# The row maxima of the first pair of sequences are spread from 16 rows instead of 128

## The reference, cut to what matters

```python
def _mlstm_parallel(q, k, v, i_pre, f_pre):
    log_fg = jax.nn.log_sigmoid(f_pre)
    lf_cs = jnp.cumsum(log_fg, axis=-1)
    lf = jnp.concatenate([jnp.zeros_like(lf_cs[..., :1]), lf_cs], axis=-1)
    log_d = lf[..., 1:, None] - lf[..., None, 1:] + i_pre[..., None, :]
    log_d = jnp.where(mask, log_d, -jnp.inf)
    m = jnp.max(log_d, axis=-1, keepdims=True)
    d_mat = jnp.exp(log_d - m)
    scores = jnp.einsum('bhtd,bhsd->bhts', q, k) * (1.0 / np.sqrt(DH))
    s_mat = scores * d_mat
    ...
x = x + _L0_xattn_ref(_layernorm(x), ctx_1024, ctx_1024, ifgate_w, ifgate_b, outnorm_w)
x = x + _L0_ffn_ref(_layernorm(x), w1_w, w1_s, w2_w, w2_s, h1_w, h1_s, h2_w, h2_s, w3_w, w3_s)
```

## Time and profile before

| | us |
|---|---|
| median of 3 runs | 836.69 |
| lowest and highest of the 3 | 834.64, 836.72 |
| the profiled execution | 834.64 |
| its span in the trace | 832.7 |
| PE busy | 807.9 (97% of the span) |
| DVE busy | 558.6 (67%) |
| ACT busy | 376.0 (45%) |
| POOL busy | 47.7 (6%) |

### The profile page before, as it was taken

The page is one execution under the profiler, slowest core; times in us unless marked ns, Lnnn a source line. Parts: engine busy times, 40 slices in busy tenths (PEclk is TensorE's granted clock), DMA queues, the critical chain, the costliest instruction groups (busy, mean ns, idle before and its releaser), DMA issues.

```text
span 832.7 us, 11915 instructions
## 1 busy us (share of the span) xinstructions
PE 807.9 (97%) x4666; PEld 687.8 (83%) x4666; DVE 558.6 (67%) x1336; ACT 376.0 (45%) x546; POOL 47.7 (6%) x53
## 2 busy tenths in 40 slices
PE   8886999999999999999999999999999999999996
PEld 6685888888888788888888888888888888888886
DVE  6865866659594785758685695858767582965543
ACT  3303544647235554546345562455545472335331
POOL 3100002000010002000020001100020000000000
PEclk9967999999999999999999999999999999999998
DMA  9922000220012100040012200031001300350540
GB/s 341 358 91 89 1 26 27 92 112 26 5 48 120 59 26 27 26 178 1 26 51 102 76 26 28 26 138 42 26 27 50 129 1 1 127 177 1 171 133 27
DMA packets 14027, 63.24 MB, mean 76 GB/s; under 512 B 1952, under 2 KB 2320, under 8 KB 11152
## 3 DMA queue, kind: packets, MB, share of 16 engines
q1 hardware_dynamic: 12672, 50.91, 17.5%
q0 software_dynamic: 1296, 11.53, 3.5%
HBM read 53.94 MB, written 8.50 MB: 75 GB/s over the span
## 4 chain that ended last, share of the span: by engine, by line
PE 79%; DVE 12%; issue 1%; ACT 1%
PE ps_f L1212 22%; PE ps_f L1213 22%; DVE decay L778 7%; PE ps_f L1188 7%; PE ps_f L1189 7%; PE ps_a L1151 6%; PE ps_f L1245 4%; PE ps_f L1246 4%; DVE decay L794 2%; PE ps_a L1131 2%; PE ps_a L1039 2%; PE ps_a L1140 1%; PE ps_a L1161 1%; PE ps_a L1102 1%; PE ps_a L1095 1%
## 5 line engine op out<-in xcount | busy, mean ns | idle before, releaser
L1212 PE MATMUL ps_f<-h_hi,wgt 128*128 128x512 f32 x1024 | 404.1, 395 | 0.0
L1213 PE MATMUL ps_f<-h_lo,wgt 128*128 128x512 f32 x1024 | 399.1, 390 | 0.0
L1212 PEld LDWEIGHTS ps_f<-h_hi,wgt 128*128 128x128 f32 x1024 | 192.4, 188 | 40.2 <-issue 0.3
L1213 PEld LDWEIGHTS ps_f<-h_lo,wgt 128*128 128x128 f32 x1024 | 192.4, 188 | 38.0
L892 DVE TENSOR_TENSOR h_lo<-work,h_hi 128x512 fp32r<-128x512 f32 x128 | 86.5, 689 | 135.0 <-ACT h_hi L597 134.0
L592 ACT ACTIVATE work<-ps_f,scl 128x512 f32<-128x512 f32 x128 | 87.5, 683 | 161.2 <-PE ps_f L1213 161.0
L1188 PE MATMUL ps_f<-h_hi,wgt 128*128 128x512 f32 x256 | 101.4, 396 | 0.0
L1189 PE MATMUL ps_f<-h_lo,wgt 128*128 128x512 f32 x256 | 100.3, 392 | 0.0
L579 ACT ACTIVATE work<-ps_f,scl 128x512 f32<-128x512 f32 x64 | 44.1, 689 | 92.8 <-PE ps_f L1189 92.8
L597 ACT ACTIVATE h_hi<-work 128x512 fp32r<-128x512 f32 x128 | 80.9, 632 | 4.1
L883 DVE SCALAR_TENSOR_TENSOR work<-ps_f,scl,work 128x512 f32<-128x512 f32 x64 | 48.0, 751 | 49.4 <-ACT work L579 49.4
(11 more groups left out here) (157 smaller groups left out, 753.5 us busy)
## 6 DMA issues: line engine op xcount, KB each, us to landing
decay<-m_rows SPq DMA_DIRECT2D x14, 1024.0 KB, 6.3
decay<-w_cols SPq DMA_DIRECT2D x22, 512.0 KB, 4.3
wgt<-w_cols POOLq DMA_DIRECT2D x5, 1024.0 KB, 13.5
v_aug<-ctx_tok SPq DMA_DIRECT2D x8, 528.0 KB, 3.6
xs<-x SPq DMA_DIRECT2D x8, 512.0 KB, 3.5
wgt<-w_cols POOLq DMA_DIRECT2D x2, 2048.0 KB, 11.9
x_kept<-xs SPq DMA_DIRECT2D x8, 512.0 KB, 2.7
out<-xs SPq DMA_DIRECT2D x8, 512.0 KB, 2.6
```

What stands on the lines that cost most here:

```text
L1212: pe.matmul(ps_f[:, bank], w, moving(h_hi[layer][:, k], as_is), start=(k == 0), stop=False)
L1213: last = pe.matmul(ps_f[:, bank], w, moving(h_lo[layer][:, k], as_is), start=False, stop=(k == KH - 1))
```

## The change

The moving operand of the 16 spreading products is now `m_row(0)`, the 16 partitions that hold maxima, and the stationary one is the first 16 rows of the identity's column. The number of products, their order, their 128 output partitions and their 256 columns stay. The clearing of `state`, its semaphore, and the two waits on it (ACT ahead of `softplus(0)`, PE ahead of the first spread) are gone.

```diff
-        s_state_clear = sem("s_state_clear")
...
             soft_cap(0)
-            act.wait_ge(s_state_clear, 1)
             softplus(0)
...
             dve.memset(rows[:], 0.0).then_inc(s_cleared, 1)
-            dve.memset(state[:, 0:2 * SEQ], 0.0).then_inc(s_state_clear, 1)
             norm_1_stats(0)
...
                     row = b * HEADS + h
-                    last = pe.matmul(spread_out(h), ident[:, row:row + 1].to_broadcast([P, P]), state[:, SEQ:2 * SEQ],
+                    last = pe.matmul(spread_out(h), ident[0:BH, row:row + 1].to_broadcast([BH, P]), m_row(0),
                                      start=True, stop=True)
...
             keep_clock(8)
-            pe.wait_ge(s_state_clear, 1)
             pe.wait_ge(s_scan, 3)
```

## The result

The changed kernel takes 842.64 us in the median of 6 runs (840.33 to 844.07), the kernel before 836.64 (834.25 to 836.74). The ratio is 1.0078, with a 95% interval of 1.0058 to 1.0098: slower by 6.0 us, where +0.3 us was forecast. The time is that of rival C (842.3 to 843.7), and lies outside the stated range.

The account below looks back on a forecast made before the run. PE, busy 97%, was taken as the bound, with the change acting only on the prologue's PE and DVE chain. Clearing 0, waits 0, stream 0 and turns +0.3 on 836.69 gave 837.0 us, range 834.2 to 839.4.

Parts of the forecast that it names:

- rival C: 16-row products let the clock fall at about 26, slowing spreads, gate products and values; 842.3 to 843.7 us, chance 0.08.
- What bounds the kernel now: Prologue: any change must show between 21.8 and 32.57 us, then passes through to the first feed-forward product.
- Parts 1 and 2, clearing and waits: Prologue: removing DVE's 0.48 us clearing, hidden by the wait for `x`, and two already satisfied waits gains 0 each.
- Part 3, the stream: Spreads: contracting over 16 rows instead of 128 leaves each record at 0.219 us start to start; 0.
- Rivals B and D: Spreads: B, exposed weight loads, 0.32 us per record, 839.0, chance 0.07; D, products abreast, 0.05, 833.8, chance 0.03.
- Part 3, the turns: Around the transposes of `rows`: two new tiling-mode turns of 0.2 us each; bounds 0 and 0.4, taken +0.3.
- the term for the clock: Spreads and gate products priced at the granted clock of before, 1.00 up to 39.7; no cost in the sum.
- A part of the array at work has not lowered it so far.: Argument against C: the clock stays 1.00 over gate products on 48 of 128 columns and scores in 32-row strips.
- The sign for C: Argument for C: the clock fell near 39.9 while PE showed one value product after another, so gapless records guarantee nothing.

Follow-up runs that it names:

- clear_on_pool: Kernel before, spreads still over 128 rows, with only the clearing of `state` moved from DVE to POOL's start; 835.38 us, ratio 0.9996.
- r16_fill8: Changed kernel plus 8 idle 128x128 products behind the eighth spread, where PE otherwise waits for DVE; 841.38 us, ratio 1.0080 to the kernel before.
- paced2: Kernel before, its 24 idle products ahead of the prologue's last transposes replaced by 39, most waiting for steps of DVE's chain; 835.45 us, ratio 0.9995.
- r16_fill8_8: Changed kernel plus 8 idle products behind the eighth spread and 8 more on the path ahead of the prologue's last gate products; 843.70 us, ratio 1.0085.

## Why the prediction was wrong

**What bounds the kernel now: right.** The path from the first spread to DVE's last masks was the one that moved, and what was added there (3.9 us) was passed on to the end without loss. Behind it, DVE hid only the low clock of the second group of scores: PE's wait ahead of the state product shrank from 1.31 to 0.39 us.

**Parts 1 and 2, clearing and waits, 0 each: right.** clear_on_pool gives 0.9996, and the 16 rows with all waits in place give the whole loss.

**Part 3, the stream, 0: right as long as the clock is up.** At the full clock, 12 records over 16 rows take 2.85 us (r16_fill8, from 22.87), over 128 rows 2.79. Rivals B and D are ruled out by it: a record starts every 0.22 us, neither 0.32 nor 0.05.

**Part 3, the turns: they exist, the size at this place was too large.** It is 0.24 us for two, where I counted 0.4 from the scores; between spreads and full idle products it is 0.38, and at the low clock some 0.56. My own rows gave less than 0.41 as well: the scores start every 0.029 us, so 32 of them are 0.93 of the 1.29 us and not 0.88, which leaves 0.36. The drain that the Trainium skill's page "TensorEngine Tiling (Array Packing)" names under Key Properties is there, and was the lesser matter. DVE's first mask came 25.08 - 22.49 = 2.59 us behind the first spread, 2.71 before, so in the trace of after they cost nothing on the path: the lower bound and not the 0.3.

**What failed is the term for the clock.** The sum has the spreads and the gate products at the granted clock of before, 1.00 up to 39.7, and puts the clock at nothing; it fell to 0.50 near 25, and that is the 6.0 us. The fall stood in the prediction only as rival C, with a chance of 0.08 and outside the range. Rival C's mechanism and its total were right: 24 records, 0.219 more for each, 5.3 us, and up to 1.4 from the values; "842.3 to 843.7" against 842.64 measured. The agreement is partly luck, because the split was different, 3.9 and 2.3 us in the trace: the wait of 1.05 us ahead of 26.75 and the return of the clock near 35 took from the first. To the second, the values gave the 1.4 as priced, and the state product at the low clock another 0.9 that was not priced. I gave it 0.08 because of one sentence: "A part of the array at work has not lowered it so far." Its two witnesses do not speak of rows. The gate products use 48 of 128 columns but all 128 rows, and the scores use strips of 32 rows, but four strips abreast, so together the whole height. No row of before shows a stretch in which PE had little but products over few rows; from 22.5 to 31.5 the changed kernel has exactly that. The absence of such a row was an open bound, and the range should have taken it in, as it did for the stream and the turns. The sign for C that I named, the fall near 39.9 during value products that left PE no gap, was weaker than it looked: it comes 2.5 us behind a gap of 1.31, and in the trace of paced2 the clock fell in that gap.

The Trainium skill's page "TensorE: Matmul & The Clock Gate", Part 1, says that the clock follows how busy PE has been recently. The trace of after disagrees if busy means what the profile counts: from 24 to 34 PE is busy 2.00 of every 2.00 us, and the clock is down.

## What to carry to other kernels

Where a stretch of a kernel has little on TensorE but a few products, cutting the rows that they contract over is not free for certain, even when these rows are zeros; here it cost 6.0 us: ask of each such stretch what holds the clock, and compare the same later instruction (here the unchanged gate products, 1.93 and 3.65 us) to see whether it held. A gap that TensorE has anyway, ahead of products that do not bring the clock back by themselves, was the cheapest place for a few full idle products: five of them in a gap of 1.3 us were worth 7.5 us by the medians (5.0 by the ratio). Here, idle products laid on the path, or run while the clock was low, brought nothing that paid for them.

## What the runs showed of the hardware that I had not expected

- Products of one shape and place, on the same data with only zeros added, kept the granted clock at 1.00 with 96 and 128 rows and lost it in the profiled executions with 16, 32 and 64. With 68 rows, three runs of ten were as long as those with 64.
- Full products of 128x128 between those of 16 rows, one to one, did not bring the clock back from 25.5 to 38.8; it came back near 42.6, behind gate products over 128 rows.
- The clock falls at different moments of the same code: at 25.9 and 23.3 in the traces of r16_fill8 and r16_fill8_8, and at 39.8 and 36.9 in those of the kernel before and paced2.
- Value products of 33 columns kept PE busy without a gap from 40 to 52 in the kernel before and did not bring the clock back; begun at the full clock behind the filled gap, all 64 records ran at it.
- A turn between products of up to 64 rows and taller ones costs 0.12 us at the full clock around the transposes and 0.19 between spreads and full idle products (0.24 and 0.38 for two), and about 0.28 at the low clock.
- The last spread over 16 rows and the first scores over 32 overlap in the trace of after, with no turn between them: the first three score records start at 36.54, the last spread record at 36.75.
